# A four-layer gated decoder: another order of the last layer's first pair, selection and sparse steps, with tokens gathered in bf16 parts

## What is computed

```python
def _L3_ffn_ref(X, ...):
    return _mosa_branch(X, router_w, wqkv, wo) + _dense_branch(X, wqkv, wo)
def _mosa_branch(X, router_w, wqkv, wo):
    scores = jnp.einsum('bth,hn->bnt', X, router_w)
    _, idx = jax.lax.top_k(scores, k)          # k = t // 8 = 64
    idx = jnp.sort(idx, axis=-1)
    gates = jax.nn.sigmoid(jnp.take_along_axis(scores, idx, axis=-1))
    Xg = jnp.take_along_axis(X[:, None], idx[..., None], axis=2)
    ...                                        # q, k, v; rope by idx; causal softmax
    out = out.at[bi, hi, idx].set(AV)
```

## Time and profile before

| | us |
|---|---|
| median of 3 runs | 493.73 |
| all runs | 493.62, 493.73, 495.23 |
| the profiled execution, time | 496.68 |
| its span in the trace | 494.9 |
| TensorE busy | 450.1 (91%) |
| VectorE busy | 279.7 (57%) |
| ScalarE busy | 220.6 (45%) |
| GpSimd busy | 111.7 (23%) |

### The profile page before, as it was taken

The page is one execution under the profiler, slowest core; times in us unless marked ns, Lnnn a source line. Parts: engine busy times, 40 slices in busy tenths (PEclk is TensorE's granted clock), DMA queues, the critical chain, the costliest instruction groups (busy, mean ns, idle before and its releaser), DMA issues.

```text
span 494.9 us, 7761 instructions
## 1 busy us (share of the span) xinstructions
PE 450.1 (91%) x3062; PEld 276.1 (56%) x3067; DVE 279.7 (57%) x588; ACT 220.6 (45%) x442; POOL 111.7 (23%) x98
## 2 busy tenths in 40 slices
PE   5999999989999899987999999989889989899986
PEld 3634443566765544776655775864345544666452
DVE  2665684486555565786235663544467753465561
ACT  3145656334102354454243325532378755467360
POOL 1300000230101103543000006000255551493300
PEclk9999999999998999999999999999999999899999
DMA  8800000270000000000000002000011111111000
GB/s 281 362 2 1 2 1 0 64 265 2 0 1 0 1 0 2 1 1 1 1 0 0 1 2 85 1 1 0 1 21 23 22 23 19 27 23 23 1 21 23
DMA packets 5493, 16.17 MB, mean 33 GB/s; under 512 B 1489, under 2 KB 2386, under 8 KB 4946
## 3 DMA queue, kind: packets, MB, share of 16 engines
q1 hardware_dynamic: 5458, 15.68, 10.3%
HBM read 13.06 MB, written 0.52 MB: 27 GB/s over the span
## 4 chain that ended last, share of the span: by engine, by line
PE 67%; DVE 18%; issue 6%; ACT 4%; POOL 3%; DMA 1%; SPq 0%; DVEq 0%; ACTq 0%; POOLq 0%
PE PS L537 57%; PE PS L1175 2%; PE PS L802 2%; DVE mxd L2200 2%; DVE mx L1762 2%; DVE wmoe L1755 2%; POOL rstd L2403 2%; PE PS L569 2%; ACT wmoe L1596 1%; DVE keys L1880 1%; PE PS L630 1%; DMA cols<-cols_dram 1%; ACT PT L1429 1%; DVE PS L2193 1%; POOL wmoe L2433 1%
## 5 line engine op out<-in xcount | busy, mean ns | idle before, releaser
L2403 POOL TENSOR_TENSOR rstd<-veps,mhalf 128x4 f32<-128x4 f32 x16 | 16.4, 1035 | 242.2 <-DVE veps L1700 242.2
L537 PE MATMUL PS<-PTB,keys 128*64 128x128 f32 (+3 forms) x384 | 41.2, 377 | 0.0
L1596 ACT ACTIVATE wmoe<-PS,mxd 128x512 f32<-128x512 f32 (+3 forms) x64 | 33.2, 534 | 4.7 <-DVE mxd L2200 4.5
L1880 DVE TENSOR_REDUCE keys<-PS 128x9 f32<-128x693 f32 x32 | 26.5, 872 | 8.6 <-PE PS L537 8.6
L1608 ACT COPY PTB<-PS 128x768 f32<-128x768 f32 (+1 forms) x24 | 20.9, 873 | 23.2 <-PE PS L1175 23.0
L537 PE MATMUL PS<-cst 128*128 128x512 f32 (+2 forms) x66 | 30.0, 566 | 0.4 <-DVE x L1720 0.4
L1374 ACT ACTIVATE sq<-PS 128x512 f32<-128x512 f32 x16 | 9.6, 598 | 44.3 <-PE PS L537 44.3
L537 PE MATMUL PS<-va,PT 128*128 128x72 f32 (+2 forms) x224 | 28.4, 277 | 1.0 <-ACT PT L1429 1.0
L537 PEld LDWEIGHTS PS<-PTB,keys 128*64 128x64 f32 (+2 forms) x384 | 20.8, 145 | 14.5 <-issue 11.6
L537 PEld LDWEIGHTS PS<-va,PT 128*128 128x128 f32 (+1 forms) x224 | 26.4, 191 | 3.0 <-ACT PT L1429 2.0
L537 PE MATMUL PS<-keys,PTB 32*128 32x231 f32 (+2 forms) x448 | 27.1, 327 | 0.3 <-DVE wmoe L1776 0.3
(11 more groups left out here) (349 smaller groups left out, 937.8 us busy)
## 6 DMA issues: line engine op xcount, KB each, us to landing
wmoe<-w_dram SPq DMA_DIRECT2D x2, 2048.0 KB, 11.8
den<-wmoe SPq DMA_DIRECT2D x28, 64.0 KB, 2.3
wa<-wa_dram SPq DMA_DIRECT2D x4, 256.0 KB, 13.4
wlate<-ew_dram SPq DMA_DIRECT2D x2, 512.0 KB, 5.3
wd<-wd_dram SPq DMA_DIRECT2D x1, 1024.0 KB, 9.2
wlate<-wm_dram SPq DMA_DIRECT2D x1, 1024.0 KB, 4.8
cst<-const_dram SPq DMA_DIRECT2D x1, 754.5 KB, 7.7
cst<-const_dram SPq DMA_DIRECT2D x1, 551.0 KB, 5.4
```

The costliest lines, as they stand in the source:

```text
L537: return nc.tensor.matmul(o, l, r, start=start, stop=stop, skip_group_check=True)
L1596: A_(PR[n % 2][:, z, to:to + (t + 1) * 128], PS[:, ring_banks("turn", n).start + z, to:to + (t + 1) * 128], ACT.Exp, bias=mxd[:, n % 2, k, ...
L1880: last = v.tensor_reduce(mxn[:, 2 * half + t, :].rearrange("p (g r) -> p g r", r=32)[:, :, 12:15], PS[:, at:at + NG, t * 256:t * 256 + GK] ...
L2403: g.tensor_tensor(rstd[:, b, :], veps[:, b, :], mhalf[:], ALU.pow).then_inc(S("ln_rstd"), 1)
```

## The change

In neutral words:

- **First pair.** VectorE multiplies the queries by cosines first, then makes the four swapped parts, then adds both q and k in one 1024-column operation; GpSimd only multiplies the keys, between the two `root` operations of the layernorm. TensorE's scores(0) stands ahead of values(0), and the `keep_clock` of two multiplications there is gone. ScalarE's copy of the fourth values stands ahead of exps(0).
- **Selection.** `top(0)` moves behind maxima(1), `top(1..3)` behind maxima(2); both `one_hots` follow "ranks" in one row.
- **Gather.** GpSimd splits the tokens into three bf16 parts (`split(0)` ahead of rope(1), `split(1)` behind rope(2), four 512-column operations each), and "gather" is 12 bf16 multiplications where it was 4 in float32.
- **Rotation.** "turns" with four 32-row copies becomes "cosines" and "sines", each two multiplications and one 128-row copy. Four memsets early in the program are gone.
- **Slots.** `FILL` places values(7), the gathers, angles, the sparse "scores", "weights", the fifth spread and "dense" elsewhere, and "y" is cut into "y0" and "y" of two multiplications each.

```diff
-        4: (("values", 7), None, ("spread", 0)),
-        6: (None, (0, "columns"), None),
+        4: (None, None, ("spread", 0)),
+        6: (("values", 7), (0, "columns"), None),
         7: ((0, "ranks"), None, None),
-        9: (None, ("spread", 1), (0, "gather")),
-        10: ((0, "angles"), (1, "gather"), (1, "angles")),
-        11: ((0, "turns"), None, (0, "q")),
+        8: (None, None, (0, "gather")),
+        9: ((0, "angles"), ("spread", 1), (1, "gather")),
+        10: ((1, "angles"), None, (0, "cosines")),
+        11: ((0, "sines"), None, (0, "q")),
         12: ((0, "k"), ("spread", 2), (0, "slots")),
         13: ((0, "v"), None, ("spread", 3)),
-        15: ((0, "scores"), None, None),
-        16: ((0, "weights"), None, ("spread", 4)),
+        15: (None, None, (0, "scores")),
+        16: (None, (0, "weights"), ("spread", 4)),
         17: ((0, "sums"), None, None),
         18: ((0, "out0"), None, (0, "out1")),
-        19: (None, (0, "dense"), None),
-        20: ((0, "y"), None, ("spread", 5)),
+        19: (None, ("spread", 5), (0, "dense")),
+        20: ((0, "y0"), None, None),
+        21: ((0, "y"), None, None),
...
-                        for t in range(TB):
-                            last = mm(PS[:, 7, :], htok[:, b * TB + t, :], OH[b][:, t, :], start=(t == 0), stop=(t == TB - 1))
+                        pe.wait_ge(S("sp_parts"), 4 * (b + 1))
+                        for n, part in enumerate(tparts[b]):
+                            for t in range(TB):
+                                last = mm(PS[:, 7, :], part[:, t * 128:(t + 1) * 128], OH[b].bitcast(BF16)[:, t, 1:1024:2],
+                                          start=(n == 0 and t == 0), stop=(n == 2 and t == TB - 1))
...
                 values(1, 7)
+                pe.wait_ge(S("d_swap"), 4)
+                scores(0)
                 pe.wait_ge(S("sp_htok"), 1)
                 values(0, 6)
-                keep_clock(3, 512, 512)
-                pe.wait_ge(S("d_swap"), 4)
-                scores(0)
                 ln_spread(7, 1)
...
+                values(3, 3, 7)
                 exps(0)
-                values(3, 3, 7)
...
+                    dve.wait_ge(S("d_raw"), 1)
+                    v.tensor_tensor(first, first, C3("ropec"), ALU.mult).then_inc(S("d_first"), 1)
                     dve.wait_ge(S("pool_set"), POOL_SET["last"])
                     dve.wait_ge(S("d_swapped"), 1)
...
-                    v.tensor_tensor(first, first, SW[0][:, 0, :], ALU.add).then_inc(S("d_first"), 1)
+                    dve.wait_ge(S("d_roped"), 1)
+                    v.tensor_tensor(both, both, SW[0][:], ALU.add).then_inc(S("d_first"), 1)
...
-                    elif s == "turns":
+                    elif s == "cosines":
                         product()
-                        for c in range(B):
-                            for j in range(2):
-                                ins = v.tensor_copy(trig[64 * c:64 * c + ROT, j, :], PS[64 * c + ROT * j:64 * c + ROT * j + ROT, 7, :])
-                        ins.then_inc(S("sp_taken"), 1)
+                        v.tensor_scalar(trig[:, 0, :], PS[:, 7, :], C3("plain"), None, ALU.add).then_inc(S("sp_taken"), 1)
+                    elif s == "sines":
+                        product()
+                        v.tensor_copy(trig[:, 1, :], PS[:, 7, :]).then_inc(S("sp_taken"), 1)
...
-                    for k in ((1, 2), (3,), (4,), (5,), (6,), (7,))[n] if n < 6 else ():
+                    for k in ((0,), (1, 2, 3), (4,), (5,), (6,), (7,))[n] if n < 6 else ():
...
+                def split(b):
+                    hi, mid, lo = tparts[b]
+                    tokens = htok[:, b * TB:(b + 1) * TB, :].rearrange("p t f -> p (t f)")
...
+                    g.tensor_copy(hi, tokens).then_inc(S("sp_parts"), 1)
...
+                    g.tensor_tensor(tokens, tokens, hi, ALU.subtract).then_inc(S("sp_parts"), 1)
...
+                    g.tensor_copy(mid, tokens).then_inc(S("sp_parts"), 1)
...
+                    g.tensor_tensor(lo, tokens, mid, ALU.subtract).then_inc(S("sp_parts"), 1)
...
+                split(0)
                 for r in range(1, PAIRS):
                     rope(r)
+                    if r == 2:
+                        split(1)
```

More of the change, by code:

```diff
@@ L167, in copied @@
     return name, before(a, name) + len(mine) * u + mine.index(j) + 1
-POOL_SET = dict(mhalf=1, first=8, iota=10, ones=18, mbias=19, mask3=20, last=26)
+POOL_SET = dict(mhalf=1, first=8, iota=10, ones=18, mbias=19, mask3=20, last=22)
 def before(a, name):
@@ L269, in constants @@
                 turns[32 * n + k, half * z + k] = 1.0
-                turns[32 * n + half + k, ROT + half * z + k] = (-1.0, 1.0)[z]
-    turns[96:98, 64] = 1.0
+                turns[32 * n + half + k, HP + half * z + k] = (-1.0, 1.0)[z]
+    turns[96:98, 2 * HP] = 1.0
+    put3("plain", p[:, None] % HP >= ROT)
     put3("turns", paired(turns))
@@ L1205, in sparse @@
                 def sparse(b, s):
-                    if s not in ("columns", "dense", "y"):
+                    if s not in ("columns", "dense", "y0", "y"):
                         pe.wait_ge(S("sp_taken"), made(b, s) - 1)
@@ L1228, in sparse @@
                                       OH[b].bitcast(BF16)[:, t, 1:1024:2], start=(t == 0), stop=(t == TB - 1))
-                    elif s == "turns":
+                    elif s in ("cosines", "sines"):
+                        at = 0 if s == "cosines" else HP
                         for c in range(B):
-                            last = mm(PS[half[c], 7, :], turns[:, 0:64], placed[c])
+                            last = mm(PS[half[c], 7, :], turns[:, at:at + HP], placed[c])
                     elif s in ("q", "k"):
@@ L1270, in sparse, with heads_out @@
                             mm(PS[:, 7, :], wod[:, q, :], AVT[:, 0, q, :], start=(q == 0), stop=False)
-                    elif s == "y":
-                        last = heads_out(0, 7, False, True)
-                    if s != "dense":
+                    elif s in ("y0", "y"):
+                        last = heads_out(0, 7, False, s == "y", *((0, 2) if s == "y0" else (2, 4)))
+                    if s not in ("dense", "y0"):
                         last.then_inc(S("last_y" if s == "y" else "sp_product"), 1)
-                def heads_out(b, bank, start, stop):
+                def heads_out(b, bank, start, stop, first=0, end=4):
                     pe.wait_ge(S("sp_taken"), made(0, "out1"))
                     pe.wait_ge(S("sp_masks"), 4 * (b + 1))
-                    for q in range(4):
+                    for q in range(first, end):
                         last = mm(PS[:, bank, :], spz[b][:, q, :], GT[b][q], start=(start and q == 0), stop=(stop and q == 3))
@@ L1294, in bank7_free @@
                         pe.wait_ge(S("x_ready"), 2 * 7 + 1)
-                    elif before7[1] != "dense":
+                    elif before7[1] not in ("dense", "y0"):
                         pe.wait_ge(S("sp_taken"), made(*before7))
@@ L2204, in rope_queries @@
                 def rope_queries():
-                    first = QK[0][:, 0, :]
+                    both = QK[0]
+                    first = both[:, 0, :]
+                    dve.wait_ge(S("d_raw"), 1)
+                    v.tensor_tensor(first, first, C3("ropec"), ALU.mult).then_inc(S("d_first"), 1)
                     dve.wait_ge(S("pool_set"), POOL_SET["last"])
@@ L2266, in masks @@
                     if b == 1:
-                        dve.wait_ge(S("sp_taken"), made(0, "turns"))
+                        dve.wait_ge(S("sp_taken"), made(0, "cosines"))
                     for q in qs:
@@ L2322, in filler @@
                 def filler(f):
-                    if f in (None, (0, "dense"), ("spread", PAIRS - 1)) or f[0] == "values":
+                    if f in (None, (0, "dense"), (0, "y0"), ("spread", PAIRS - 1)) or f[0] == "values":
                         return
@@ L2334, in final_layer @@
                 maxima(0)
-                top(0)
                 for n in range(NS):
@@ L2349, in final_layer @@
                     if n == 7:
-                        one_hots(0)
-                    elif n == 8:
-                        one_hots(1)
+                        for c in range(B):
+                            one_hots(c)
                     elif n == 16:
```

47 lines of the change are left out of this document (21 added, 26 removed).

## The result

| | median, us | all runs, us |
|---|---|---|
| before | 493.68 | 493.30, 493.62, 493.73, 495.23 |
| after | 486.22 | 485.02, 485.80, 486.64, 488.26 |

The ratio after/before is 0.9856, with a 95% interval of 0.9822 to 0.989: faster by 7.5 us in the medians, where 9.9 was forecast. The profiled execution of after took 486.64, with a span of 484.8; before it was 494.9.

The account below looks back on a forecast made before the run. TensorE, busy 91% of the span, was taken as the bound, gaining only from waits, less work or clock. Terms -4.6 - 0.5 - 6.2 + 0.7 - 1.1 + 1.8 = -9.9 us took 493.73 to 483.8, range 480.9 to 489.5.

Parts of the forecast that it names:

- First pair: Last layer up to scores(3): scores(0) and scores(3) start earlier, with the rope next late; -4.6 us.
- Values(7): Up to scores(9): its 0.94 us leaves round 4 and fills round 6's wait of 0.93; -0.5 us.
- Scores(9) to scores(15): Shorter gathers, waits gone in round 9, at the gather and at "q", no clock fall; -6.2 us.
- Sparse scores and weights: Scores(15) to scores(18): the chain from turn(15) through sparse scores and "weights" takes 14.7 us, before 14.03; +0.7 us.
- Scores(18) to scores(22): Half of "y" leaves, 1.88 us; new waits at "out1" and "dense" taken as 0.8; -1.1 us.
- "y" in round 21: Scores(22) to turn(23): the other half of "y" stands there and the chain behind keeps its length; +1.8 us.
- The waits take the gains back: Rival: no gain in round 4, weaker gathers, one new clock fall, dearer waits at "out1" and "dense"; 488.4 us, chance 0.25.
- The sentence on micro-idles: Cited skill rule: micro-idles between matmul groups can swing TensorE's clock; by it alone each new wait could cost 1.5 us.
- GpSimd as the bound: Rival: splits delay rope(1) and rope(3); slower than before from 3.3 us an operation, 499.4 us at 4.0; chance 0.03.
- It does not do what it says: Rival: the first pair gains nothing since scores(3) waits for something else; -5.3 us, 488.4 us, chance 0.05.
- brackets over 1.5 us in rounds 8 to 20: Sign of being wrong: TensorE waits longer than 1.5 us in those rounds of the last layer.
- Turn(23): Sign of being right: this TensorE step near the end of the last layer starts about 9.9 us earlier.

Follow-up runs that it names:

- The last experiment: Changed kernel with ScalarE widening pair 5's reciprocals, plus sparse "scores" two slots earlier and their exponentials behind exps(16); 482.55 us, ratio 0.9779.
- the second: Changed kernel with no edit, traced once more and timed again; 485.37 us, ratio 0.9842, layer 140.00 us.
- the kernel with the clock held: Changed kernel with two unread 512-column multiplications on TensorE ahead of `spread(5)`; 485.54 us in one run, layer 141.40.

## Why the prediction came out as it did

**Sum.** The range, 480.9 to 489.5, held 486.22; the forecast of 483.8 was 2.4 us too low. In span it forecast 485.0 and 484.8 came, but that is partly luck: 3.6 of those 10.1 us lie ahead of the layer, and the layer gained 6.5.

**First pair, forecast -4.6, measured -4.1.** Scores(0) was forecast 7.0 into the layer and stands at 7.10; the 1024-column addition took 1.22 (forecast 1.25). The splits took 0.61, 1.15, 0.61 and 1.16, 3.75 from the first start at 347.16 to the last end (forecast 3.6), and cost nothing: the kernel without them has scores(3) at the same place. The rope was next late, as forecast. The product that makes h of batch 1 was forecast 9.7 into the layer and starts at 9.77 (348.69); the 0.5 too much lies between it and scores(3). Of the 4.1, the pair alone gives 3.3; the tops, which the prediction only used to clear ScalarE's way, give 0.8.

**Values(7), forecast -0.5, measured -0.25.** Right in kind: the wait of 0.93 in round 6 is gone and round 4's turn waits 0.58.

**Scores(9) to scores(15), forecast -6.2, measured -6.4.** The pieces that were measured came close: two gathers -1.6 (forecast -1.7), "q" waits 0.56 (0.5), the copies take 0.75 and 0.68 (0.70), the brackets in round 9 and at the gather are gone, and the clock stays up. One thing was taken for certain that isn't: a wait of 2.66 us at "q" need not bring the clock down, as the kernel with pair and tops shows. The 1.5 us stood in both traces of before, so the term is right for them.

**Sparse scores and weights, forecast +0.7, measured +0.9.** The chain of three VectorE operations and ScalarE's exponentials is exposed by 1.35 us at "weights". The last experiment gets 1.8 back.

**Scores(18) to scores(22), forecast -1.1, measured +1.75: the step that failed.** It read: "new waits come at "out1" and "dense"" and "Bounds for these 0 and 2.4; I take 0.8". With half of "y" (1.88) out of the interval, the new cost was 3.6 in the profiled execution of after, over the upper bound, and 0.93 in the second, near the value taken. The place was wrong too: at "dense" there is 0.26 or 0.70, at "out1" 0.43 as before (0.44); what was missing is the wait of `spread(5)` for VectorE to empty the bank. The term counts maxima(20) and `norm` ahead of "dense" and puts pair 5's copy at nothing, as if its time were fixed. It isn't: the copy has 0.58 us of room, and held by GpSimd's rope(7) it takes up to 2.65. That costs 1.7 in the profiled execution, and the clock's fall behind the wait 1.0; together they are the 2.7 between the two executions. The copy stood at the same place in before, with the same room, so the change did not bring the risk, and the term missed what before's trace shows in little, in the row of 0.82. It was not among the rows that I took.

**"y" in round 21, forecast +1.8, measured +1.7.** The cut as a whole is worth 0.6 against "y" in one piece.

**Rivals.** "The waits take the gains back" came true in one of its parts, the clock falling once in a new place, and at another size. The sentence on micro-idles stands in the Trainium skill, TensorE: Matmul & The Clock Gate, under "A second HAM failure mode: psum-queue depth-cycling" and not under "HAM oscillation". The prediction set it aside with "by the rows none does", for waits up to 1.67 us. That bound held at the steps of the last layer (1.66, 1.51 and 1.43 brought no fall), but the new wait was 1.83, outside it. It was also read from the last layer alone: in before's first trace the clock fell at 150 us behind no wait over 0.69 in the 30 us ahead of it. GpSimd as the bound fell: 0.61 and 1.16 for an operation, where 2.1 was the point at which it begins to cost. "It does not do what it says" fell. One of the prediction's own signs of being wrong, "brackets over 1.5 us in rounds 8 to 20", came: it is the 1.83. Turn(23) is 10.0 us earlier in the span, as forecast, but by the same luck: 6.5 of them in the layer.

**What the medians say.** With the layer's start at 339.3, where it must be for a median of before of 493.5, the medians of after, 486.2 and 485.4, leave layers of 141.9 and 141.2 us, between the two timings 142.7 and 140.0. That fits a copy that is held in part of the executions, and as well one that is always held while the clock seldom falls (141.4 in the kernel with the clock held). It is an estimate, not seen, since only profiled executions have a trace.

## What to carry to other kernels

Look at what an operation runs beside, not only at what it waits for. A VectorE copy from SBUF to SBUF beside a GpSimd operation costs what is left of that operation, here up to 2.2 us. If the two start within tenths of each other, and one of them waits for a DMA, the kernel has two timings, and one trace shows only one of them: take a second trace before a difference of 1 to 3 us is given to an edit. Give such a copy to ScalarE when it has room, or let one engine wait for the other. For a float32 operand multiplied by exact 0/1 selections, three bf16 parts made on an idle engine cut 3.60 us to 2.80.
